# The lone node's constant row is added by GpSimd instead of VectorE for the last 11 of 38 pairs

## What is computed

```
x = layernorm(x + L0(x, edges))      # softmax aggregation, two-layer MLP
x = layernorm(x + L1(x, edges))      # sum aggregation, MLP, batch norm over all nodes
x = layernorm(x + L2(x, edges))      # h[src] * filter summed by dst, MLP
x = layernorm(x + L3(x, edges))      # two layers of mean aggregation
```

## Time and profile before

| | us |
|---|---|
| runs | 2345.66, 2338.79, 2345.47 |
| median | 2345.47 |
| the profiled execution | 2339.05 |
| its span | 2337.3 |
| VectorE busy | 1995.1 (85%) |
| TensorE busy | 2070.5 (89%) |
| ScalarE busy | 1785.9 (76%) |
| GpSimd busy | 1276.0 (55%) |

### The profile page before, as it was taken

How to read it: one execution, slowest core, us unless ns; L and a number is a source line. 1 busy time by engine, 2 the same in 40 slices (tenths; PEclk the granted TensorE clock), 3 DMA queues, 4 the chain that set the end, 5 groups by cost and what they waited for, 6 DMA issues and landing times. The chain is left out here.

```text
span 2337.3 us, 45661 instructions
## 1 busy us (share of the span) xinstructions
PE 2070.5 (89%) x14016; PEld 1727.8 (74%) x14017; DVE 1995.1 (85%) x2947; ACT 1785.9 (76%) x3691; POOL 1276.0 (55%) x1115
## 2 busy tenths in 40 slices
PE   5999999999999799998999688888799999687662
PEld 4999999999999577776677577777567777566552
DVE  7999999999998566665999699999789999689664
ACT  4989888999988477776777488888689999577321
POOL 5766655665640333331485587740056665477676
PEclk9999999999999899999899899999899999899887
DMA  3656565555565788886897589876446667477751
GB/s 113 165 159 160 150 160 161 168 162 166 177 190 164 202 250 255 255 253 193 204 222 182 124 200 208 196 191 167 134 139 207 195 203 231 129 211 200 221 182 61
DMA packets 256985, 427.17 MB, mean 183 GB/s; under 512 B 50849, under 2 KB 103252, under 8 KB 256746
## 3 DMA queue, kind: packets, MB, share of 16 engines
q1 hardware_dynamic: 210028, 367.21, 52.7%
q0 software_dynamic: 46400, 56.69, 12.7%
q10 hardware_dynamic: 318, 0.36, 0.0%
HBM read 240.16 MB, written 186.37 MB: 182 GB/s over the span
## 5 line engine op out<-in xcount | busy, mean ns | idle before, releaser
L523 PE MATMUL banks<-mats,g_hT 128*125 128x256 f32 x1000 | 258.9, 382 | 0.0
L542 PE MATMUL banks<-mats,g_zT 128*125 128x128 f32 x2000 | 238.8, 273 | 0.0
L542 PEld LDWEIGHTS banks<-mats,g_zT 128*125 128x125 f32 x2000 | 228.2, 188 | 0.0
L1824 POOL DMA_INDIRECT acc<-combined,first_ x100 | 174.7, 1747 | 72.9 <-issue 30.5
L523 PEld LDWEIGHTS banks<-mats,g_hT 128*125 128x125 f32 x1000 | 189.3, 189 | 27.8 <-issue 0.2
L1887 POOL DMA_INDIRECT em_y<-acc,from_ x100 | 112.3, 1123 | 174.5 <-PE banks L2035 144.6
L868 POOL DMA_INDIRECT gin_xs<-x,from_ x100 | 98.7, 987 | 186.2 <-DMA x_of_src<-gin_xs 161.0
L1043 DVE TENSOR_TENSOR gin_acc<-gin_acc,gin_qr 125x512 f32<-125x512 f32 x125 | 86.7, 693 | 119.2 <-ACT gin_qr L1003 119.2
L603 ACT ACTIVATE g_zT<-banks,cols 128x500 f32<-128x500 f32 x250 | 179.2, 777 | 2.0 <-PE banks L531 2.0
L445 POOL DMA_INDIRECT g_xd<-in_x,idx x100 | 100.3, 1003 | 139.9 <-PE banks L557 115.5
L586 ACT ACTIVATE g_sq<-banks 125x512 f32<-125x512 f32 x250 | 144.1, 591 | 37.8 <-PE banks L523 35.5
(11 more groups left out here) (419 smaller groups left out, 6548.3 us busy)
## 6 DMA issues: line engine op xcount, KB each, us to landing
acc<-g_zero SPq DMA_DIRECT2D x126, 224.0 KB
x<-g_x SPq DMA_DIRECT2D x125, 224.0 KB
g_x<-in_xT SPq DMA_DIRECT2D x100, 250.0 KB
h<-gin_hr SPq DMA_DIRECT2D x50, 448.0 KB
al_h<-h SPq DMA_DIRECT2D x38, 448.0 KB
al_x<-x SPq DMA_DIRECT2D x38, 448.0 KB
out<-al_out SPq DMA_DIRECT2D x38, 448.0 KB
gin_x<-x SPq DMA_DIRECT2D x37, 448.0 KB
```

The source lines that it names most:

```text
L523: m = nc.tensor.matmul(bank[0:P, 256 * j:256 * j + 256], HT[q % 2][:, c:c + P], K.W1c, start=False, stop=j == 1)
L542: m = nc.tensor.matmul(pO[q % 2][0:P, D * j:D * j + D], ZT[q % 2][:, h, P * j:P * j + P], K.W2[:, h, :], start=False, stop=j == R - 1 and ...
L1824: pool.indirect_dma_start(out=K.acc, out_offset=bass.IndirectOffsetOnAxis(ap=K.first_all[:, g, r:r + 1], axis=0), in_=CR_all[:, g, r * D:r ...
```

## The change

For pairs 27 to 37 `add_alone` is taken out of VectorE's list and put at the end of GpSimd's, behind `side`. The instruction, its tiles and its semaphores are the same.

```diff
+BY_POOL = 27
...
-    def add_alone(self, dve, k):
-        if k < self.count:
-            past(dve, self.x2, k)
+    def add_alone(self, eng, k):
+        if k < self.count:
+            past(eng, self.x2, k)
             alone = self.K.alone[0:P, :].rearrange("p (o d) -> p o d", o=1).to_broadcast([P, 2 * R, D])
-            self.nc.vector.tensor_tensor(self.B[k % 2][:, :, :], self.B[k % 2][:, :, :], alone, ALU.add).then_inc(self.b, 1)
+            eng.tensor_tensor(self.B[k % 2][:, :, :], self.B[k % 2][:, :, :], alone, ALU.add).then_inc(self.b, 1)
...
-            block.gpsimd(side)
+            @block.gpsimd
+            def _(pool):
+                side(pool)
+                for k in range(BY_POOL, count):
+                    n.add_alone(pool, k)
...
-                steps(count, [(1, on(n.apply_a, dve)), (1, on(n.add_alone, dve)), (3, on(n.apply_c, dve)), (0, on(n.residual, dve, 0)),
+                steps(count, [(1, on(n.apply_a, dve)), (1, lambda k: n.add_alone(dve, k) if k < BY_POOL else None), (3, on(n.apply_c, dve)), (0, on(n.residual, dve, 0)),
```

## The result

| | before | after |
|---|---|---|
| runs on the same chips | 14 | 14 |
| median us | 2338.82 | 2348.64 |
| from - to | 2334.67 - 2345.66 | 2338.97 - 2353.65 |
| profiled execution | 2339.05 | 2343.62 |

What follows compares the result with a forecast made beforehand. VectorE is full, but the add is a link of a chain within one step: steps of 10.07 instead of 9.34 us cost 7.3, the end 1.3, together 8.5 on the median 2345.47, so 2354 us; range 2344 to 2362.

Steps and rivals of the forecast that it cites:

- The mechanism: Within a node-pass step, reduce_b waits for square_b, which waits for GpSimd's add; VectorE's 1.25 us relief becomes waiting.
- The level: Whole kernel: 2354 us, forecast from the three runs' median of 2345.47; chance 0.53.
- The step: Pairs 27 to 37: 4.85 us to reduce_b plus 5.22 to the next apply_a, 10.07 instead of 9.34.
- The add: On GpSimd, 1024 elements a partition: taken as 2.2 us, between 1.05 and 2.79.
- the handovers: VectorE to GpSimd 0.25 us (0.04 to 0.84), GpSimd to ScalarE 0.10 (0.04 to 0.24).
- The end: Last pair running through alone: square_b starts 3.77 us after apply_a, not 2.51, so 1.3 us more.
- the sum of 8.5: Node pass: ten steps costing 7.3 us plus 1.3 at the end, together 8.5 us slower, rounded down.
- VectorE's wait: VectorE idle about 2 us before reduce_b in each changed step, released by square_b.
- Quick enough to hide: Rival, before reduce_b: an add of 1.47 us leaves the step unchanged; a loss below 7.0 needs under 2.07; chance 0.32.
- The floor: With a short add, ScalarE's order from reduce_b through exp_a and square_b binds the step at 9.17 us.
- In each other's way: Rival: GpSimd's add holds up apply_c and a residual, 0.55 us a step more, 14.5 slower, 2360; chance 0.10.
- A first add that starts late: Rival, before pair 27's add: late gathers or a one-off start-up of 6 us give 2360; chance 0.05.

Runs made afterwards that it cites:

- the ladder: Changed kernel, but GpSimd adds only 8, 8, 7, 6, 5, 4, 3, 2, 1, 1 and 1 of a pair's 8 rows; 2341.63 us, a single run.
- the run with one row: Changed kernel, but GpSimd adds only 1 of a pair's 8 rows in all eleven pairs; ratio 0.9997 to the kernel before.
- the four with their later stages moved: Changed kernel with square_b onward one step later: alone 1.0026; also reordered 0.9991; reordered, all adds on VectorE 1.0004; reordered, 21 adds on GpSimd, later stores 0.9928 (repeat 0.9926).

## Why the prediction was right

**The mechanism** was as predicted, link by link: reduce_b is released by square_b, square_b by the add, and VectorE's relief turns into waiting. The experiments show it rather than argue it: the step follows the add's length one for one down to 9.19 us, and it shrinks back when the link gets a step of slack.

**The level.** 2354 was worked out from the median of three runs, 2345.47; fourteen runs give 2338.82 for the kernel before, 6.65 less. The forecast as a ratio, 2354/2345.47 = 1.0036, is what was measured; the two medians differ by 9.82 us, 1.3 more than the sum said. So the 5.4 us between 2354 and 2348.64 are the base that was 6.65 too high, less those 1.3.

**The step**: 10.07 predicted, 10.00 measured. The add takes 2.36 where I took 2.2 (0.16 more); the handovers take 0.08 and 0.03 where I took 0.25 and 0.10 (0.24 less). The select and the transfer that I bounded the handover by the earlier trace rows were both too dear; the lower end of my range was the right neighbour. Ten steps cost 6.33 us, not 7.3, also because one of the ten took 9.61 in the kernel before.

**The add.** Its length is 0.18 us + 2.13 ns a number (455 ns for 128 numbers, 2361 for 1024). The fixed part is that of the select; the slope is 2.5 times the select's 0.85 ns, more than two reads one after the other would give (1.70); what the rest is isn't shown. My 2.2 was two such reads (1.92) with 0.28 for losses; the losses are 0.44, and the add lies midway between 1.92 and 2.79, not near 1.92. The Trainium skill (GPSIMD Engine Reference, section 3.1, Elementwise — side-by-side cycle accounting) gives 4497 ns for 2048 numbers, by which 2.20 ns a number is an estimate; the trace, with 2.13, agrees.

**The end**: 1.3 us predicted, 2.04 measured. square_b of the last pair starts 3.67 us after apply_a (1673.97 - 1670.30) instead of 2.51, so 1.16 of it is the add (1.26 in the sum). The other 0.88 is a cause that the prediction didn't have: TensorE is late with the pair ahead, at a lower clock (last section). So the sum of 8.5 against 8.35 owes its closeness in part to luck, to two misses that cancel: steps 1.0 too dear, the end 0.7 too cheap.

**VectorE's wait.** About 2 us ahead of reduce_b was predicted. It came in two places: 1.17 ahead of reduce_b and 0.57 ahead of apply_c, which now comes up before ScalarE's exp_c is done. That second wait was not foreseen. It costs nothing, as reduce_b has to wait for longer than that behind it.

**The rivals.** *Quick enough to hide* decides at an add of 1.47 us by the prediction; in the ladder the step is back at 9.36 with 1.54 and 9.18 with 1.27; the add took 2.36. The floor that the prediction read from ScalarE's order, 9.17, is the 9.18 to 9.19 of the short adds, term by term (2.98, 1.58, 3.55 and 1.08 from 1596.15 to 1605.34 in the run with one row). That run gives 2.55 us for the most that could be had: 1.49 in the ten steps (the prediction's 1.7 lay there), 0.86 at the end with an add of 0.45, and 0.20 in steps that the change doesn't touch. *In each other's way* is out: apply_c and the residual beside the add take 1.23 and 0.68, as without it, and apply_c waits for ScalarE. The Trainium skill (SBUF — State Buffer, Who interferes with whom) says that VectorE contends with a GpSimd instruction that reads SBUF where it reads two inputs from SBUF itself; these two read one of theirs from PSUM, and the trace agrees. *A first add that starts late* is out by the 18.03 us above.

## What to carry to other kernels

An engine that is 99% busy isn't relieved by taking an instruction off it if that instruction is a link of a chain which comes back to the engine within the same step: then the link's latency counts, down to the next bound (here 9.18 us a step, 0.17 below the full engine's), and a slower engine lengthens it. Before moving such work, find the next instruction of the full engine that depends on it; if it lies within the step, move it to the next step first (software pipelining), and only then hand the work to the slower engine. Here eleven such adds lost 8 us in the old order, and 21 of them, spread over a pipelined one, belong to a kernel that is 0.7% faster, in which each is worth about 0.50 us a step.

## What the runs showed of the hardware that wasn't expected

**TensorE's clock in the drain.** From the busy times by stretch of after, behind the last apply_a; the granted clock is the last column but two:

```profile
1668.00:1672.00 4.00, 2.62 (x10) 1.34 (x10) 4.00 (x5) 2.94 (x7) 0.40 (x1) 0.80 0.86 230
1672.00:1676.00 4.00, 3.14 (x7) 1.69 (x7) 1.59 (x2) 2.34 (x3) 1.94 (x1) 0.50 1.07 246
```

and of the kernel before, the first of these two stretches:

```profile
1668.00:1672.00 4.00, 3.42 (x23) 2.64 (x24) 3.39 (x4) 2.13 (x4) 0.00 (x0) 1.00 1.04 282
```

The two products of a pair that fall into the slow stretch, from the timeline of after and then of before:

```profile
1670.45 2.04 PE L1337 MATMUL banks<-al_x3T,mats 128*128 128x500 f32 x2 [1.19 <-ACT al_x3T L1365]
...
1673.35 2.01 PE L1337 MATMUL banks<-al_x3T,mats 128*128 128x500 f32 x2 [0.86 <-ACT al_h3T L1372]
```

```profile
1666.02 1.11 PE L1336 MATMUL banks<-al_x3T,mats 128*128 128x500 f32 x2 [1.19 <-ACT al_x3T L1364]
...
1667.98 1.08 PE L1336 MATMUL banks<-al_x3T,mats 128*128 128x500 f32 x2 [0.86 <-ACT al_h3T L1371]
```

A clock of 0.50 is the lower of TensorE's two levels (1.2 of 2.4 GHz), and the products take almost twice as long, 1.9 us more for the two. They belong to the pair before the last. TensorE is still busy with it when the last pair's apply_b is done, so that turn_x3 comes late, as the timelines of after and then of before show:

```profile
1676.89 1.23 DVE L1442 TENSOR_TENSOR al_b<-al_b,al_nb_r 125x1024 f32<-125x1024 f32 x1 [0.61 <-ACT al_nb_r L1243]
...
1678.77 1.02 PE L1329 MATMUL banks<-ident,al_b 125*128 125x125 f32 x8
```

```profile
1671.31 1.23 DVE L1441 TENSOR_TENSOR al_b<-al_b,al_nb_r 125x1024 f32<-125x1024 f32 x1 [0.61 <-ACT al_nb_r L1242]
...
1672.59 1.07 PE L1328 MATMUL banks<-ident,al_b 125*128 125x125 f32 x8
```

That is 1.88 us after apply_b instead of 1.28; copy_x3 follows 1.12 after that (1679.89) instead of 0.86 (1673.45), and the two make 0.86 of the 0.88 at the end. The pause of 1.19 us ahead of the first product is the same in both kernels. In the stage ahead TensorE had been busy for 74.53 of 90 us instead of 79.90. Among the profiles the clock fell at this place in the two kernels whose steps were 10.0 us long (after, and the adds from pair 22 on, with 0.73 and 0.84 in two stretches of 4 us at this place); in the kernel before, the ladder, the run with one row, and the four with their later stages moved it stayed at 1.00 until TensorE's last products were through, with steps of about 9.3 or less ahead. That the emptier stage causes the drop goes with these profiles; it wasn't tested by itself. If it does, a chain that lengthens a step costs a second time, on an engine that is no link of it.

**GpSimd's transfers beside VectorE.** The last 16 transfers that GpSimd issues in the pass fetch the next stage's inputs. In after, such an instruction took 0.94 to 0.96 us or 1.83 to 1.91. One of each, with the instruction of VectorE that had just begun:

```profile
1548.12 1.22 DVE L1442 TENSOR_TENSOR al_b<-al_b,al_nb_r 125x1024 f32<-125x1024 f32 x1
1548.28 1.89 POOL L1892 DMA_INDIRECT em_y<-acc,from_  x1 [0.30 <-issue]
...
1550.40 1.22 DVE L1232 TENSOR_REDUCE al_nc_s<-al_nc_sq 125x8 f32<-125x1024 f32 x1
1550.47 0.94 POOL L1892 DMA_INDIRECT em_y<-acc,from_  x1 [0.30 <-issue]
```

All six long ones began beside apply_a or apply_b, which read two tiles in SBUF; the ten short ones began beside a reduce, a residual or apply_c, or in the last 0.14 us of an add. In the run with adds from pair 22, all 16 were issued while VectorE stood still and took 0.94 to 0.95. So GpSimd was through with its transfers 231.55 us after the pass's first apply_a (1546.85 - 1315.30), in after 237.24 (1553.57 - 1316.33): 5.7 us sooner, although VectorE had stopped, and six times 0.93 is 5.6. That beginning beside such an instruction is what doubles the time fits all of these transfers; it wasn't tested by itself. It is the saving that the expectation of that run allowed for: the pass lost 35.5 us where about 38 was expected.
